# A convolution and attention kernel on one core: fp32 scores on row tiles of TensorE, exponentials over four PSUM banks, softmax sums out of the value product

## The reference

```
x = conv_block(x)                         # graph mixing, 1x1 and temporal convolutions, relu, residual
t = tokens(x)                             # [32, 400, 32]
n = layernorm(t)
Q, K, V = (n @ rot) @ Wq.T, (n @ ent) @ Wk.T, n @ Wv.T
dist2 = sum(Q*Q)[:, :, None] + sum(K*K)[:, None, :] - 2 * Q @ K.T
t = t + softmax(exp(-dist2)) @ V          # so two exponentials for each score
u = layernorm(t) @ W.T, normalised over all batches and tokens
y = sigmoid(u_t + y @ V.T), step by step  # t = t + y, back to [32, 32, 16, 25]
```

## Time and profile before

| what | us |
|---|---|
| median of 3 runs (lowest, highest) | 223.04 (221.67, 223.66) |
| the profiled execution | 221.07 |
| its span, first to last instruction | 219.2 |
| convolution stage, to the first `center` of the last pair | 0 to 75.5 |
| last pair, with the first group's scores | 75.5 to 94.3 |
| attention of groups 1 to 7 | 94.3 to 177.6 |
| last layernorms and statistics | 177.6 to 190.0 |
| batch statistics, recurrence, output | 190.0 to 219.2 |

### The profile page before, as it was taken

The page is one execution under the profiler, slowest core; times in us unless marked ns, Lnnn a source line. Parts: engine busy times, 40 slices in busy tenths (PEclk is TensorE's granted clock), DMA queues, the critical chain, the costliest instruction groups (busy, mean ns, idle before and its releaser), DMA issues. The chain is left out here.

```text
span 219.2 us, 3489 instructions
## 1 busy us (share of the span) xinstructions
PE 193.8 (88%) x1171; PEld 98.4 (45%) x1171; DVE 160.7 (73%) x298; ACT 170.3 (78%) x323; POOL 29.8 (14%) x44
## 2 busy tenths in 40 slices
PE   6858999999999969699999999999999998479950
PEld 6633646546546435323243343434333423259840
DVE  0649369999999944996876695968777795675990
ACT  4073799699699799988988989899999974286740
POOL 7000000370150080260203010101010000000000
PEclk9999999999999999969999999999999999997995
DMA  6940200276349150591534435170800000000016
GB/s 176 374 154 21 74 2 0 49 273 165 88 167 240 41 224 22 213 228 31 134 100 123 108 81 147 40 189 4 212 14 3 0 0 0 0 3 3 0 67 235
DMA packets 20213, 21.95 MB, mean 100 GB/s; under 512 B 2046, under 2 KB 17086, under 8 KB 20068
## 3 DMA queue, kind: packets, MB, share of 16 engines
q1 hardware_dynamic: 20196, 21.73, 33.8%
HBM read 14.74 MB, written 6.96 MB: 99 GB/s over the span
## 5 line engine op out<-in xcount | busy, mean ns | idle before, releaser
L507 ACT ACTIVATE arena<-ps 128x800 f32<-128x800 f32 (+1 forms) x56 | 44.6, 798 | 5.8 <-PE ps L1064 5.4
L514 ACT ACTIVATE arena<-arena 128x800 f32<-128x800 f32 (+1 forms) x56 | 46.4, 830 | 0.0
L1064 PE MATMUL ps<-qa,ka 128*128 128x400 bf16 (+1 forms) x128 | 35.5, 341 | 2.0 <-ACT arena L507 1.9
L1064 PE MATMUL ps<-qb,kb 96*128 96x400 bf16 (+1 forms) x128 | 35.5, 339 | 0.0
L741 DVE TENSOR_TENSOR psum<-arena 128x400 f32<-128x400 f32 x32 | 19.6, 611 | 14.2 <-ACT arena L514 14.2
L741 DVE TENSOR_TENSOR psum<-psum,arena 128x400 f32<-128x400 f32 x32 | 19.5, 608 | 6.1 <-ACT arena L514 4.7
L1064 PEld LDWEIGHTS ps<-qa,ka 128*128 128x128 bf16 (+1 forms) x128 | 10.4, 98 | 26.2 <-ACT arena L507 13.7
L1097 PE MATMUL ps<-arena,vb 128*32 128x400 f32 x192 | 21.6, 525 | 0.3 <-issue 0.3
L750 DVE RECIPROCAL arena<-ps 128x400 f32<-128x400 f32 x7 | 18.5, 2649 | 0.0
L1182 PE MATMUL ps<-yb,cst 128*128 128x120 f32 (+1 forms) x102 | 16.6, 309 | 1.7 <-ACT yb L597 1.4
L660 DVE COPY arena<-arena 32x400 f32<-32x400 f32 x48 | 17.2, 358 | 0.9
(11 more groups left out here) (151 smaller groups left out, 353.8 us busy)
## 6 DMA issues: line engine op xcount, KB each, us to landing
ka<-dk SPq DMA_DIRECT2D x32, 100.0 KB
qa<-dq SPq DMA_DIRECT2D x32, 100.0 KB
dk<-arena SPq DMA_DIRECT2D x8, 300.0 KB, 2.2
dq<-arena SPq DMA_DIRECT2D x8, 300.0 KB, 2.7
arena<-x_tok SPq DMA_DIRECT2D x4, 400.0 KB
t<-x SPq DMA_DIRECT2D x1, 1600.0 KB, 11.3
kb<-dk SPq DMA_DIRECT2D x16, 100.0 KB
qb<-dq SPq DMA_DIRECT2D x16, 100.0 KB
```

Of the source, the lines that this page charges most:

```text
L507: nc.scalar.activation(prob[par][:, lo:hi, :], ps[:, o:o + hi - lo, 0:N], ACT.Exp, scale=2.0).then_inc(e1_done, 1)
L514: nc.scalar.activation(p, p, ACT.Exp).then_inc(p_ready, 1)
L1064: last = mm_(ps[row:row + keys, bank, 0:N], kk[par][0:rows, b, o:o + keys], qq[par][0:rows, b, :], start=first, stop=not first, skip_group ...
```

## The change

The scores are computed in fp32 from K and Q as they are. `kf` and `qf` hold 32 channels of 4 batches on 4 x 32 partitions. `scores(g, q)` takes key tile q (of 3, `FULL`) of all four batches: four fp32 matmuls with 32 rows each, on row tiles 0, 32, 64 and 96 of the array, into banks 0 to 3, and four bf16 matmuls with 6 rows (`ek`, `eq`: three parts of each squared norm against ones). `tail_scores` does the last 16 keys into bank 4. ACT reads all four banks in one 128x1600 instruction. There is one set of four banks, so `scores` waits for `e1_done` of the unit just before it. For a group that makes three wide units and a tail.

The split in bf16 parts, its DRAM round trip and `ka`, `kb`, `qa`, `qb` go. SP sends the squared norms from SBUF to SBUF instead, 16 small DMAs a pair. The values are multiplied by the identity instead of `wvT`; the 32nd column of each tile is set to ones, so that `products` gives the softmax sum as its last row. DVE copies the product (`unscaled`), and `mix_values` multiplies by `w2`, which holds `wvT` with the missing channel worked in. For groups 0 to 5 the sum row is stored to DRAM and read back by four broadcast DMAs (`spread_sums` of SP), and DVE takes the reciprocal of that; for groups 6 and 7 a matmul spreads it. `add_tiles`, `sums`, `tail_sums` go. The square of `norm2` goes to DVE (`squares2`, two instructions) for groups 0 to 5. Two of the eight tap copies of a group go from ACT to POOL. Ten fillers instead of three. `outs` shares the memory of `kf`.

```diff
-FILLS_FIRST = 3
+FILLS_FIRST = 10
-UNITS = (TILES + 1) // 2
+UNITS = FULL + 1
...
+            def spread_sums(g):
+                sp.wait_ge(us_ready, g + 1)
+                sp.dma_start(scaled[g], us[:, :]).then_inc(sums_out, 16)
+                sp.wait_ge(sums_out, 16 * (g + 1))
+                if g > 0:
+                    sp.wait_ge(rden_ready, g)
+                for b in range(NB):
+                    sp.dma_start(sums[C * b:C * b + C, :],
+                                 scaled[g, C * b + C - 1:C * b + C, :].partition_broadcast(C)).then_inc(sums_in, 16)
...
+            def tap_inputs(i):      # in the POOL block
+                if i > 1:
+                    pool.wait_ge(e_ready, i - 1)
+                for par in range(2):
+                    pool.wait_ge(zp_ready, 2 * i + par + 1)
+                    for k in POOL_TAPS:
+                        last = nc.gpsimd.tensor_copy(*tap_input(par, 1, k))
+                    last.then_inc(u_pool, 1)
...
+            def inner(g, q):
+                act.wait_ge(s_done, FULL * g + q + 1)
+                nc.scalar.activation(prob[g % 2][:, NB * q:NB * q + NB, :], ps[:, 0:NB, 0:N], ACT.Exp,
+                                     scale=2.0).then_inc(e1_done, 1)
...
+            def scores(g, q):
+                if q == 0:
+                    pe.wait_ge(k1_ready, g + 1)
+                    pe.wait_ge(q1_ready, g + 1)
+                    pe.wait_ge(e_in, 16 * E_LOADS * (g // 2 + 1))
+                if FULL * g + q:
+                    pe.wait_ge(e1_done, FULL * g + q)
+                for b in range(NB):
+                    mm_(ps[:, b, 0:N], kf[C * b:C * b + C, g, P * q:P * q + P], qf[C * b:C * b + C, g, :],
+                        start=True, stop=False)
+                for b in range(NB):
+                    r = slice(C * b, C * b + 2 * EP)
+                    last = mm_(ps[:, b, 0:N], ek[r, g, P * q:P * q + P], eq[r, g, :], start=False, stop=True)
+                last.then_inc(s_done, 1)
...
+            def unscaled(g):
+                dve.wait_ge(pv_done, g + 1)
+                if g > 0:
+                    dve.wait_ge(w2_done, g)
+                    if g < G - 1:
+                        dve.wait_ge(sums_out, 16 * g)
+                nc.vector.tensor_copy(us[:, :], ps[:, PV_BANK, 0:N]).then_inc(us_ready, 1)
...
             for g in range(1, G):   # in the DVE block
+                if g > 1:
+                    reciprocals(g - 2)
+                    quotient(g - 2)
+                    residual(g - 2)
+                if g > 2:
+                    project2(g - 3)
+                    stats(g - 3)
+                unscaled(g - 1)
+                if g > 1:
+                    squares2(g - 2)
```

More of the change, by code:

```diff
@@ L559, in _ @@
-            for step, first, end in ((squares, 0, 2), (inverse_roots, 2, 3), (kq_firsts, 3, 5),
-                                     (v_and_squares, 5, UNITS)):
-                step(PAIRS - 1)
-                for u in range(first, end):
-                    inner(0, 0, u)
-                    if u:
-                        outer(0, 0, u - 1)
+                inner(g, 0)
+                inner_tail(g - 1)
+                outer(g - 1, 2)
+                outer_tail(g - 1)
+                if g > 2:
+                    norm2(g - 3, 1)
+                    norm2(g - 3, 2)
@@ L566, in _ @@
+                inner(g, 1)
+                outer(g, 0)
+                inner(g, 2)
+                outer(g, 1)
+            squares(PAIRS - 1)
+            inner(0, 0)
+            inverse_roots(PAIRS - 1)
+            inner(0, 1)
+            outer(0, 0)
+            kq_squares(PAIRS - 1)
+            inner(0, 2)
+            outer(0, 1)
+            e_copies(PAIRS - 1)
             for g in range(1, G):
-                weights(g, g % 2)
-            outer(G - 1, 1, UNITS - 1)
+                weights(g)
@@ L1100, in center2 @@
[L1100 to L1112 removed]
+                    o = slice(C * b, C * b + C)
@@ new lines, in mix_values, with center2 @@
+            def mix_values(g, bank=SUM_BANK):
+                if g == 0:
+                    pe.wait_ge(w2_ready, 1)
+                elif g == G - 2:
+                    pe.wait_ge(rden_ready, g + 1)
+                elif bank == SUM_BANK:
+                    pe.wait_ge(nrm_ready, g)
+                pe.wait_ge(us_ready, g + 1)
+                mm_(ps[:, bank, 0:N], w2[:, :], us[:, :], start=True, stop=True).then_inc(w2_done, 1)
+            def center2(g, bank=NORM_BANK):
+                pe.wait_ge(t1_ready, g + 1)
+                if g > 0 and bank == NORM_BANK:
@@ new lines, in _ @@
+            tail_scores(0)
+            pe.wait_ge(es_ready, G)
+            pe.wait_ge(rows_ready, 2)
+            mm_(ps[:, SUM_BANK, 0:P], rest[:, :], c_("wvT"), start=True, stop=True).then_inc(w2_made, 1)
+            products(0, 0)
+            pe.wait_ge(wc_ready, 1)
+            for g in range(1, G):
+                scores(g, 1)
+                if g > 2:
+                    variance2(g - 3)
+                products(g - 1, 1)
+                if g > 1:
+                    mix_values(g - 2)
+                if g > 2:
+                    project2(g - 3)
+                scores(g, 2)
+                products(g - 1, 2)
+                tail_products(g - 1)
+                if g < G - 1:
+                    scores(g + 1, 0)
+                tail_scores(g)
+                if g == G - 1:
+                    spread_sums(g - 1)
+                if g > 1:
+                    center2(g - 2)
+                products(g, 0)
```

569 lines of the change are left out of this document (226 added, 343 removed).

## The result

The changed kernel takes 230.64 us in the median of 4 runs (229.75 to 232.2); the kernel before took 222.35 us on the same chip (220.5 to 223.66). The ratio is 1.039, with a 95% interval of 1.034 to 1.044. I had forecast 215.0 us, with a range of 207 to 225. It is slower, and outside the range. The profiled execution is one of 230.86 us with a span of 228.8.

What follows compares the result with a forecast made beforehand. PE was taken to bound the convolution stage and ACT the attention stage, each with another engine close behind. Terms -9.5 - 4.6 + 1.5 + 5.0 - 0.5 = -8.1 us on 223.04 gave 215.0 us, range 207 to 225.

Steps and rivals of the forecast that it cites:

- The second ring, through DRAM: Attention loop: sums' store, loads, reciprocal and DVE passes take 10.9 us a turn with 2 us of slack, adding nothing.
- the end: Group 7's start to the statistics: 29.0 us instead of 24.0, +5.0 us, through the order of DVE's queue.
- the first ring: Attention loop: scores and first exponential alternate on one set of banks, through PE and ACT, 11.0 us a group.
- The price of a unit (U): PE's scores in the attention loop: four row tiles cost as much as one, 1.0 us a unit.
- A: Rival on PE's scores: row tiles' weight loads follow each other, U 1.4 to 1.5, 224 to 226 us; chance 0.13.
- B: Rival on PE's scores: fp32 row tiles don't run together, U 3.8, some 290 us in all; chance 0.06.
- The exponentials: ACT in the attention loop: 1600 wide, 1.38 and 1.44 us each; merging banks saves 0.4 us a group.
- the loop's later turns: Attention loop after the early groups: four turns of 11.0 us each, against 12.0 before.
- the last pair: Centre of the last pair to group 1's first exponential: 14.3 us instead of 18.9, -4.6 us.
- Convolution stage: PE stays the bound; POOL's tap copies slow DVE, +1.5 us in the first pair, 0 in each later turn.
- Recurrence: After the statistics: seven more fillers cost nothing and full clock gives 0 to 1.7 us; -0.5 us taken.
- C: Rival in the attention loop: the DRAM round trip takes 7 instead of 5.2 us, +8, 223 us; chance 0.08.

Runs made afterwards that it cites:

- act_taps_alone: The changed kernel with GpSimd's tap copies back on ScalarE and nothing else undone: 226.04 us, ratio 1.019 to the kernel before.
- Experiments 1 and 2: 1 is sums_ahead; 2 is the changed kernel with every group's sums spread by a matmul, none through DRAM: 219.42 us, ratio 0.990.
- sums_ahead: The changed kernel with the last pair's entropy transfers issued four at a time behind the stores of groups 0 to 3: 219.63 us, ratio 0.991.
- experiment 3: sums_ahead with GpSimd's tap copies back on ScalarE: 218.43 us, ratio 0.989.
- experiments 9 and 12: 9: experiment 3 plus early sums copy, group 5's square on ScalarE, three fillers for ten: 215.03 us; 12: that, centre ahead of products, no fillers: 214.61 us.

## Why the prediction was wrong, point by point

**The step that failed** is "The second ring, through DRAM", with its "So I add nothing". It counted the trip as store, load and issue of the sums' own transfers, and not what stands on SP ahead of the first store. The entropies' transfers, sixteen for a pair with 0.67 us an issue, were priced nowhere. They hold the first store back by 8.8 us; ACT loses 11.07 us in one wait. The rest goes with the clock, as far as one pair of profiles can say: in act_taps_alone, with the store as late, the stall is 2.4 us shorter. Experiments 1 and 2 each take the stall away without removing a transfer of entropies, and give back 11 us. With the queue in that order and the rest as it was, the changed kernel would have been 219.6 us, within my range and just within 1% of the kernel before (ratio 0.991). Its profiled execution stands 6.6 us above the 213.0 of my sum; 1.9 of that are in the loop and 3.9 at the end.

**The ring through DRAM, its steady state.** I had it at 10.9 us with 2 us of slack. In sums_ahead a round takes 11.1 to 12.0 us, in the changed kernel behind the stall 11.3 to 13.1, and the slack is used up. It costs little in the loop, since the first ring is 11.26 and the stall had left DVE some room. But it puts the copy of group 6's sums at 12.6 us behind group 7's first exponential (181.62), where I had 10.5. That is most of the 2.3 us by which the end was longer than forecast. The order at the end, which I had as dear, is so:

```profile
184.99 2.65 DVE L706 RECIPROCAL arena<-ps 128x400 f32<-128x400 f32 x1
...
191.02 0.57 DVE L695 COPY us<-ps 128x400 f32<-128x400 f32 x1 [0.39 <-PE ps L1051]
```

The reciprocal of group 6 at 15.95 us (forecast 13.75) and the last copy at 22.0 (19.75): the same chain, 2.2 us late.

**The price of a unit (U)**, the open one, was right: 1.0 forecast, 1.05 measured from start to start. The timeline of PE answers to the earlier trace rows:

```profile
137.75 0.95 PE L1017 MATMUL ps<-qf,kf 32*128 32x400 f32 x8
138.52 0.35 PE L1021 MATMUL ps<-eq,ek 6*128 6x400 bf16 x4
138.80 0.94 PE L1081 MATMUL ps<-sq,cst 128*128 128x400 f32 x2
```

Four fp32 row tiles take 0.77 us, as long as one full matmul, and four bf16 tiles 0.28 and not 0.17. Rivals A and B fall. (A's price for a load, 0.11 us, is what the trace of the kernel before has for 32 columns of fp32; for 128 columns it has 0.19. Eight of those would be 1.5 us, so in the 0.77 us of L1017 they overlap.) The Trainium skill (TensorE: Matmul & The Clock Gate, Part 3: Packing small matmuls) gives 3.07 times for four row tiles; these rows show four in the time of one, 4 x 0.77 / 0.77.

**The exponentials** were right: 1.38 to 1.40 us from start to start for the first and 1.43 for the second (1.38 and 1.44 forecast). So were **ACT's pace in the early groups** (9.33, forecast 9.1), **the loop's later turns** (11.26, forecast 11.0) and **the last pair** (14.8, forecast 14.3).

**Convolution stage.** Forecast +1.5; the profile after shows +3.9. But sums_ahead has the same code there and is 2.1 us shorter, all of it in the first pair, without the stretches at half clock from 7.5 and 17.7 us on. So the change is worth +1.8 us, and experiment 3 gives 2.0 back: GpSimd's copies, as I had argued, but not where. In the first pair they cost 0.8 us, where I had 1.5, and in each of the three later turns 0.4, where I had nothing. What they took from DVE in the first pair was less than I thought: 0.9 us (3.13 against 2.23) beside four copies of 0.65 us. The Trainium skill (SBUF — State Buffer, on the shared port pair) has one of the two blocked until the other's instruction ends. By that DVE would lose up to an estimated 4 x 0.65 = 2.6 us; it lost a third of this. That the earlier trace rows showed 1.31 us for one addition is one collision, not the rule for six short copies.

**Recurrence.** Forecast -0.5, by fewer microseconds at half clock. The profile after has 3.4 us at 1.2 GHz all the same, and 0.7 us less in the stage. The stretch came earlier, counted from the aggregate: 6.2 us behind it before (196.3 to 199.7, on the steps), 1.7 us behind it after (202.0 to 205.4, on the priming matmuls and the fillers). So the first step is 0.8 us later (5.09 against 4.25 behind the aggregate), and the steps behind it run at full clock. That the sign agrees is luck. My seven fillers at 0.11 us took 0.21 each, and whether the fillers or chance moved the stretch isn't shown: with the same number of them the stage differs by 1.0 us (experiments 9 and 12).

**The rivals.** C was the nearest: it named the trip through DRAM, priced at a longer landing for each group. The trip itself was not the cause: in sums_ahead, behind the copy's end, it takes 5.3 to 6.6 us, where I had 5.2 and C 7, and the loop is 64.1 us. The cause was one late store. None of my cases had a stall that occurs once. 0.15 on slower was too little, with a ring that I had called as long as the first and a queue that I had not written out.

## What to carry to other kernels

When a transfer is added to an in-order queue, write out that queue at the moment of its first use, with a price for each issue, and not only the trip of the transfer itself. A small transfer isn't a cheap issue: sixteen of 2.3 KB held the queue for 10.9 us, 0.67 each, where the store of 200 KB took 0.35 to 0.42. Where two rings have nearly the same length, expect an edit to one of them to show nothing, and test it again with the other one open. Read a fall of the clock as a second bill behind a long wait. And before a difference of a microsecond in one stage is given to an edit, look how far that stage differs between profiles that have the same code there.

## What I had not expected of the hardware

An issue of a three-row transfer from SBUF to SBUF takes 0.67 us on SP, a load of 50 KB from DRAM spread over 32 partitions 0.43 (1.72 for four), and a load of three rows from DRAM in the kernel before 0.31. That the form of the transfer makes the difference is my reading; no run here changed the form alone.

The clock after the stall: at 1.2 GHz from 116.7 to 130.4 us in the profile after, so that the turn of the stall and what followed paid 1.7 us for what takes 0.95. I can't say why it came back at 121.0 in act_taps_alone and only at 130.4 here.

Early in the program TensorE shows half clock in some executions and not in others, with the same instructions. The windows from 20 to 25 us, first of the changed kernel, then of sums_ahead (PE busy, clock):

```profile
20.00:25.00 5.00, 5.00 (x9) 0.55 0.01 3
```

```profile
20.00:25.00 5.00, 4.02 (x38) 1.00 0.01 3
```

In both PE had idled 3.19 us ahead of the first pair's taps. With a shorter stretch from 7.5 to 10.9 us, which sums_ahead lacks too, it moves the stage by about 2 us from one profile to the next. What decides it stays open, and one profile alone would have put it down to the change.
